# Attention behind a group norm: the first batch's keys as centred input, the scale folded into weights and z

## The reference

```python
xg = x.reshape(B, 4, C // 4, H, W)
y = ((xg - mean(xg)) * rsqrt(var(xg) + 1e-5)).reshape(B, C, N) * gamma + beta
q, k, v = split(w_qkv @ y + b_qkv, 3)
scores = q.T @ k * C ** -0.5
out = x + w_out @ (softmax(scores) @ v.T).T + b_out
```

## Time and profile before

| | us |
|---|---|
| median of 3 runs | 136.11 |
| lowest, highest | 136.02, 136.78 |
| the profiled execution | 135.91 |
| its span, first to last instruction | 134.1 |
| PE busy | 129.0 |
| DVE busy | 100.1 |
| ACT busy | 74.8 |
| POOL busy | 73.0 |

### The profile page before, as it was taken

One profiled execution on the slowest core, in us unless ns is written; L12 is line 12 of the kernel. 1 busy time (PEld: TensorE's weight loads), 2 busy tenths in 40 slices (PEclk: granted clock), 3 DMA queues, 4 the chain that ended last, 5 costly groups with the idle time before them and its releaser, 6 DMA issues.

```text
span 134.1 us, 1876 instructions
## 1 busy us (share of the span) xinstructions
PE 129.0 (96%) x579; PEld 91.1 (68%) x579; DVE 100.1 (75%) x191; ACT 74.8 (56%) x131; POOL 73.0 (54%) x78
## 2 busy tenths in 40 slices
PE   6999999999999999999999999999999999899991
PEld 6877687777777566666765656776665676558890
DVE  0598686999999999769788785698886826759121
ACT  3164768775588655656753284576732545868000
POOL 6133166589458877963386678933493355142600
PEclk9999999999999999999999999999999999999999
DMA  4950000000039808596799458963898299902111
GB/s 158 332 215 0 0 5 0 0 2 0 0 78 207 187 0 196 131 210 175 163 210 209 122 117 194 215 185 86 191 209 221 51 209 210 229 9 78 39 65 52
DMA packets 6874, 16.63 MB, mean 124 GB/s; under 512 B 1873, under 2 KB 2129, under 8 KB 6865
## 3 DMA queue, kind: packets, MB, share of 16 engines
q1 hardware_dynamic: 6576, 16.26, 49.4%
q10 hardware_dynamic: 288, 0.27, 0.6%
HBM read 2.36 MB, written 2.10 MB: 33 GB/s over the span
## 4 chain that ended last, share of the span: by engine, by line
PE 73%; DVE 9%; POOL 7%; issue 4%; DMA 2%; ACT 1%; POOLq 0%; DVEq 0%
PE mixed L847 22%; PE scores L793 8%; PE scores L794 8%; PE scores L796 8%; DVE scores L592 4%; PE turned L810 4%; POOL probs L334 4%; PE turned L740 3%; DVE crossed L619 3%; DMA xs<-in_x_dram 2%; PE mixed L849 2%; POOL y_lo L310 2%; PE mixed L740 1%; DVE stats L518 1%; PE mixed L844 1%
## 5 line engine op out<-in xcount | busy, mean ns | idle before, releaser
L334 POOL TENSOR_SCALAR probs<-probs,inv_sum 128x1024 f32<-128x1024 f32 x32 | 35.9, 1122 | 42.0 <-DVE inv_sum L597 41.9
L592 DVE TENSOR_SCALAR_CACHE_REDUCE scores<-scores,key_bias 128x1024 f32<-128x1024 f32 x31 | 40.0, 1289 | 11.5 <-PE scores L796 11.5
L421 ACT ACTIVATE probs<-scores,neg_max 128x1024 f32<-128x1024 f32 x32 | 35.7, 1116 | 20.0 <-DVE scores L592 19.2
L847 PE MATMUL mixed<-crossed,v 128*128 128x512 f32 x84 | 39.5, 592 | 0.0
L793 PE MATMUL scores<-y_hi,z_hi 128*128 128x512 f32 x62 | 34.5, 557 | 0.1
L619 DVE STREAM_TRANSPOSE crossed<-probs 128x1024 f32<-128x1024 f32 x24 | 29.8, 1242 | 1.4 <-POOL probs L334 1.2
L794 PE MATMUL scores<-y_lo,z_hi 128*128 128x512 f32 x62 | 24.4, 394 | 0.0
L847 PEld LDWEIGHTS mixed<-crossed,v 128*128 128x128 f32 x84 | 15.1, 190 | 11.0 <-issue 10.1
L796 PE MATMUL scores<-y_hi,z_lo 128*128 128x512 f32 x62 | 19.3, 392 | 0.0
L793 PEld LDWEIGHTS scores<-y_hi,z_hi 128*128 128x128 f32 x62 | 11.7, 189 | 8.5 <-issue 5.7
L794 PEld LDWEIGHTS scores<-y_lo,z_hi 128*128 128x128 f32 x62 | 11.7, 189 | 7.0 <-issue 5.5
(11 more groups left out here) (159 smaller groups left out, 179.5 us busy)
## 6 DMA issues: line engine op xcount, KB each, us to landing
crossed<-crossed SPq DMA_DIRECT2D x92, 128.0 KB, 2.3
out_dram<-result SPq DMA_DIRECT2D x7, 256.0 KB, 2.4
xs<-in_x_dram SPq DMA_DIRECT2D x2, 512.0 KB, 6.7
xs<-in_x_dram SPq DMA_DIRECT2D x3, 256.0 KB, 4.8
xs<-in_x_dram ACTq DMA_DIRECT2D x1, 256.0 KB, 3.3
ws<-in_weights_dram SPq DMA_DIRECT2D x1, 256.0 KB, 3.6
out_dram<-result SPq DMA_DIRECT2D x2, 128.0 KB, 1.9
vecs<-in_vectors_dram ACTq DMA_DIRECT2D x1, 3.0 KB, 3.8
```

What stands on the lines that cost most here:

```text
L334: pool.tensor_scalar(probs[:, i % RING, :], probs[:, i % RING, :], inv_sum[:, i:i + 1], 1.0, ALU.mult, ALU.mult).then_inc(s_probs, 1)
L421: act.activation(probs[:, i % RING, :], scores[:, i % 2, :], ACT.Exp, bias=neg_max[:, i:i + 1], scale=-1.0, accum_out=row_sum[:, i:i + 1]) ...
L592: dve.tensor_scalar(scores[:, i % 2, :], scores[:, i % 2, :], key_bias[:, b % 2, i:i + 1], None, ALU.subtract, ALU.min, accum_out=neg_max[ ...
L847: mm = pe.matmul(bank, v[:, b % 2, k, :], at, start=first, stop=final)
```

## The change

For batch 0 alone, z and the scores no longer use the normalised input but c = x less its channel mean. The normalised input is norm_a * c + shift, where shift = norm_a * (channel mean less group mean) + beta. Of z = G y + z_bias the scale on the input side goes into the fold (`first_fold_hi`, `first_fold_lo`: the fold times norm_a along its rows), the shift's product with the fold into the bias, and the scale on the key side into z, which is multiplied by norm_a as ACT copies it (`scale=norm_a`, `first_z_bias`). So the heads of the keys need only the channel means. The key bias of batch 0 gets a column of its own in `wv_out` (C + 1, from `first_key_vector`) and a scalar of its own (`first_bias_score`), since the queries' side changes with the shift; PE gets four one-column products for this (lines 978, 989, 999, 1007 of the new kernel), DVE and ACT some one-column instructions. The values are still made of the normalised input y: ACT makes 384 columns, POOL 640.

The z tail of the second half stands between the second normalisation and the input of batch 1. The core of the diff (lines unchanged in kind are left out):

```diff
@@ gpsimd @@
-            pool.tensor_scalar(minus_mean[:, :], group_mean[:, :], -1.0, None, ALU.mult).then_inc(s_const, 1)
...
+            pool.wait_ge(s_c1, 1)
+            pool.wait_ge(s_c_hi, 2)
+            pool.wait_ge(s_c_lo, 2)
+            pool.tensor_tensor(y_lo[:, 0, second], y[:, 0, second], y_hi[:, 0, second].bitcast(fp32),
+                               ALU.subtract).then_inc(s_c_lo_rest, 1)
...
+            first_z_tail(1, FIRST, HALF)
             pool.wait_ge(s_norm, 1)
+            pool.wait_ge(s_c_lo_rest, 1)
+            pool.tensor_scalar(y[:, 0, 3 * 128:N], xs[:, 0, 3 * 128:N], norm_a[:, 0:1], norm_b[:, 0:1],
                                ALU.mult, ALU.add).then_inc(s_y0_rest, 1)
...
+            pool.tensor_tensor(fold_lo[:, :], fold[:, :], fold_hi[:, :].bitcast(fp32), ALU.subtract).then_inc(s_fold_lo, 1)
             normalise(0, 0)
             rstd_of(1, 2, 2)
             normalise(0, 1)
+            first_z_tail(2, HALF, N)
@@ scalar @@
+            act.wait_ge(s_centre, 1)
+            for half in (slice(0, HALF), slice(HALF, N)):
+                act.activation(y_hi[:, 0, half], xs[:, 0, half], ACT.Identity, bias=centre[:, :]).then_inc(s_c_hi, 1)
             act.wait_ge(s_folded, 1)
+            act.activation(fold[:, :], setup[:, SET_G:SET_G + C], ACT.Copy, scale=-SCALE).then_inc(s_fold, 1)
...
+            act.wait_ge(s_folded, 3)
+            act.activation(wv_out[:, 0:C], setup[:, SET_V:SET_V + C], ACT.Copy).then_inc(s_setup, 1)
+            act.wait_ge(s_fold, 1)
+            act.wait_ge(s_scale, 1)
+            act.activation(first_fold_hi[:, :], fold[:, :], ACT.Identity, scale=norm_a[:, 0:1],
+                           bias=blank[:, 0:1]).then_inc(s_first_fold_hi, 1)
...
             def first_values(job, bank):
                 act.wait_ge(s_v0, V_NO[job] + 1)
+                act.wait_ge(s_key_bias, V_NO[job] + 1)
                 value_copy(0, job, bank)
@@ vector @@
+            dve.tensor_scalar(centre[:, :], mean_var[:, 0, 0:1], -1.0, None, ALU.mult).then_inc(s_centre, 1)
+            channel_spreads(0, 1, mixed[:, 1, :])
...
+            centred_tail(1, slice(0, FIRST))
             variances(0, 1, 1, mixed[:, 1, :])
...
             def first_key_biases(job, bank):
-                dve.wait_ge(s_v, V_NO[job] + 1)
+                dve.wait_ge(s_v0, V_NO[job] + 1)
@@ tensor @@
-                pe.matmul(minus_means[:, MINUS_MEAN + lo:MINUS_MEAN + hi], minus_mean[:, :],
-                          mean_var[:, lo:hi, 0], start=True, stop=True).then_inc(s_gmean, 1)
...
+            pe.wait_ge(s_fold, 1)
+            pe.matmul(setup[:, SET_Z:SET_Z + 1], wqk[:, 1, :], BQ, start=True, stop=True).then_inc(s_folded, 1)
...
-            keep_warm(3)
+            keep_warm(2)
...
+            pe.matmul(mixed[:, 1, first], first_fold_hi[:, :], c_hi[:, first], start=True, stop=False)
+            pe.matmul(mixed[:, 1, first], first_fold_hi[:, :], c_lo[:, first], start=False, stop=False)
+            pe.wait_ge(s_first_fold_lo, 1)
+            pe.matmul(mixed[:, 1, first], first_fold_lo[:, :], c_hi[:, first], start=False, stop=True).then_inc(s_z0, 1)
```

More of the change, by code:

```diff
@@ new lines, in _ @@
+            act.wait_ge(s_first_biases, 1)
+            act.activation(wv_out[:, C + 1:C + 2], mixed[:, 0, FIRST_U:FIRST_U + 1], ACT.Copy, scale=SCALE).then_inc(s_setup, 1)
+            act.activation(z_full[:, FIRST:HALF], turned[:, 0, FIRST:HALF], ACT.Identity, scale=norm_a[:, 0:1],
+                           bias=first_z_bias[:, :]).then_inc(s_z0_full, 1)
+            act.wait_ge(s_first_biases, 2)
+            act.activation(first_bias_score[:, :], mixed[:, 1, FIRST_S:FIRST_S + 1], ACT.Copy, scale=SCALE).then_inc(s_setup, 1)
@@ L479, in _ @@
             exponentials(0, 1)
+            act.wait_ge(s_z0_tail, 1)
+            act.activation(z_full[:, :], mixed[:, 1, :], ACT.Identity, scale=norm_a[:, 0:1],
+                           bias=first_z_bias[:, :]).then_inc(s_z0_full, 1)
             for b in range(BATCHES):
@@ L902, in _ @@
[L902 to L907 removed]
+            c_hi, c_lo = y_hi[:, 0, :], y_lo[:, 0, :]
@@ L916, in _ @@
[L916 to L921 removed]
+            pe.matmul(to[0], z_hi[:, 0, first], c_hi[:, halves[0]], start=True, stop=False)
@@ new lines, in _ @@
+            pe.wait_ge(s_c_hi, 2)
+            pe.matmul(to[1], z_hi[:, 0, first], c_hi[:, halves[1]], start=True, stop=False)
+            pe.wait_ge(s_c_lo, 2)
+            pe.matmul(turned[:, 0, left], first_fold_hi[:, :], c_lo[:, left], start=False, stop=True).then_inc(s_z0, 1)
+            pe.matmul(to[0], z_hi[:, 0, first], c_lo[:, halves[0]], start=False, stop=False)
+            pe.wait_ge(s_first_key, 1)
+            pe.matmul(mixed[:, 0, FIRST_U:FIRST_U + 1], wqk[:, 0, :], first_key_vector[:, :], start=True,
+                      stop=True).then_inc(s_first_biases, 1)
```

279 lines of the change are left out of this document (159 added, 120 removed).

## The result

| | before | after |
|---|---|---|
| median of 6 runs each, us | 136.50 | 139.48 |
| lowest, highest | 136.02, 136.78 | 139.19, 140.60 |
| ratio, after to before | | 1.0239 (1.0201 to 1.0277) |
| the profiled execution, us | 135.91 | 140.60 |
| its span | 134.1 | 138.8 |

The changed kernel is 2.4% slower: 3.3 us by the ratio, 3.0 by the medians. The forecast was 136.5 with 137.3 as its upper bound. With three more runs the kernel before has a median of 136.50, where the forecast was worked out from 136.11. All ratios here are the record's; they leave out runs more than 1.5% above the fastest of the same kernel: 139.53 of the first experiment, 138.02 of the last but one, and of the kernel before one at 166.5 with a mean clock of 0.755.

What follows compares the result with a forecast made beforehand. The prediction saw an opening of dependent steps, then full DVE and PE queues from DVE's maximum of block 5 at 25.98 us. +0.87 − 0.19 − 0.22 = +0.46 gave 136.5 us, range 135.3 to 137.3.

Steps and rivals of the forecast that it cites:

- the sum: Whole kernel: +0.87 at block 5's maximum, −0.19 and −0.22 given back later, +0.46 us in all.
- the hinge: DVE's maximum of block 5, at 25.98 us before; delay there passes almost whole to the end; forecast 26.85, +0.87.
- step 5: Behind block 5's maximum: DVE's wait at 40.88 goes, −0.19 us, and the mean product at 60.06 goes, −0.22.
- the rival on the clock: PE idles about 0.75 before the setup products; its clock falls, some 1.5 us more, 138; chance 0.05.
- Step 1: Setup to first z: PE waits for the fold copy; first z product at about 9.15 against 8.83, 0.3 late.
- Steps 2 and 3: First scores, values, first exponential: last score product and first values 0.5 late, block 1's maximum about 0.65; earlier exponential buys nothing.
- Step 4: Blocks 2 to 5: value copies wait for the key bias, exponentials behind them; block 5's maximum +0.87 us.
- The first rival: Opening: scaled fold not held by setup products, all up to first z 0.65 earlier; 135.4 to 135.7; chance 0.2.
- The second: Blocks 2 and 3: exponentials held twice by ACT's V1 and V2 copies behind the key bias; +0.95, 137.1; chance 0.25.

Runs made afterwards that it cites:

- the first experiment: Changed kernel with three warming products ahead of PE's wait for the fold copy, against the kernel before: median 137.17 us, ratio 1.0049.
- the last but one: Kernel before with the later means subtracted, plus the first exponential ahead of the first value copy: 135.93 us, ratio 0.9969 against the kernel before.
- the warm kernel: Changed kernel plus one warming product where the second mean product stood and three ahead of the fold wait: 137.01 us, ratio 1.0045 against the kernel before.
- both moves on ACT: Changed kernel, fold copied between key halves, scaled fold ahead of the value-weight copy, warming products filling pauses: 136.48 us, ratio 0.9994 against the kernel before.
- V1 and V2 freed: Kernel with both moves on ACT and PE kept warm, only its first value copy still behind the key bias: 136.17 us, ratio 0.9980 against the kernel before.
- one short pause: Kernel with both moves on ACT, without the two warming products ahead of the fold wait: 139.11, 139.19, 138.96 and 136.03 us.

## Why the prediction was wrong

**The verdict.** Wrong, by a step that it named and priced away. Kept warm throughout, the change costs 0.45% (0.25 to 0.65), 0.6 us (0.8 by the medians), where the sum said 0.46. The other 1.9%, 2.6 us, goes with the half clock. It isn't a property of this change: the kernel before loses 2.4 us by a pause, 1.8 of them beyond the delay. That the sum comes so near the warm kernel is partly luck: at the hinge that kernel is 1.34 late and not 0.87, and behind it more is given back than the 0.41 of step 5.

**The step that failed: the rival on the clock.** The text said that PE would idle for about 0.75 before the setup products, that a fall of the clock there would make products up to about 11 us take twice as long, 1.5 us, and that "nothing in the trace speaks for it", and gave it a chance of 0.05. The pause came as written, 0.79. The chance was wrong: all 6 runs of the changed kernel had the half clock, and pauses of 0.34 to 0.55 brought it too. The price was wrong as well, 1.5 us where 2.6 were lost: the half clock lasted to 17.9 us in the profiled run, over the scores, the values and the next block's first product, and for 6.9 us in the shorter runs, which is past 14 if it fell where it did here. The reasoning took "granted clock is 1.00 in all stretches" as a sign that the clock is safe. The stretches of the earlier trace rows begin at 26 us and say nothing of the opening; the page does show 9 in every slice, but only for a kernel in which PE hardly pauses there. What did speak for the danger stood in the same trace: ten warming products in front and three in the middle keep PE fed, and its longest pause there is 0.19.

**Step 1** had the right string and sized it short: the first z was to be 0.32 late, and kept warm it is 0.81 late. (A slip in its sum has no weight: with 0.70 each and an overlap of 0.1 the halves end at 6.93, not 6.96.) The key halves were no part of the error: 0.70 was expected of each, and the group of them in the changed kernel (count, busy us, mean ns) reads

```profile
L492 ACT ACTIVATE y_hi<-xs,first_negated_means 128x512 fp32r<-128x512 f32 x2 | 1.3, 712 | 0.0
```

By the rule of the Trainium skill, "ScalarE: Activation LUTs", section "What ACT_TABLE_LOAD costs", it would be 0.71; the trace agrees. The five products started at 7.41 (7.2 expected). The extra warming products stand in the 0.81, since they end behind the fold copy (8.27 against 7.91), and the runs don't part the two. With both moves on ACT the scaled fold starts at 8.65.

**Steps 2 and 3** hold as differences. From the first z to the last score product the warm kernel loses 0.10 more, the first values add nothing, block 1's maximum 0.2 more; the text had 0.2, 0.0 and 0.15. That the earlier exponential buys nothing is shown by the kernel that has it alone.

**Step 4.** From block 1's maximum to the hinge the warm kernel loses 0.23, the text had 0.22. The place is right too: block 3's exponential runs to 25.85 there and PE's scores of block 5 start at 25.99, 1.06 behind the turning ahead of them, where the old opening takes 0.85 (23.84 to 24.69). With V1 and V2 freed it is 0.85 again (23.75 to 24.60), and 0.26 comes back at the hinge of that profile.

**Step 5.** The removed mean products give 0.54 us (0.34 to 0.76) in the old kernel, for 0.41. Beside that kernel, which has them removed as well, the warm one is 1.34 late at the hinge and 1.2 at the end of the span (135.5 against 134.3). In the changed kernel the hinge is 5.1 late and the span 4.7 longer, and the reciprocal no longer waits.

**The first rival** (the opening flies) fell: the fold copy held PE, as the text said against it. **The second** (exponentials held twice, 137.1) has its time by chance near the warm kernel's 137.01, but not its mechanism: block 1's maximum was already 1.1 late, and block 2's exponential ends at 22.67, before PE is ready for block 4's scores at 23.23, so only one exponential holds PE.

**What is left.** The best of the kernels here is the old opening with the later means subtracted, 0.996 (0.9944 to 0.9975). With both moves, no pause and free value copies the new opening reaches 0.998 (0.9962 to 0.9998), so of the forms tried here none pays beyond the subtraction that it brings.

## What to carry to other kernels

Before adding a wait to TensorE near a kernel's start, look up its longest pause there so far, and treat any longer one as a danger to the clock, not as free idle time: here pauses of 0.34 to 0.79 us made kernels 2.4 to 3.3 us slower in most runs, the delay itself included. Fill the wait with products on a blank tile: the same delay with the pause filled cost 0.6 us in place of 2.4. A clock that reads 1.00 everywhere speaks for the present order, and says nothing about the next.

## What the hardware showed

**Short pauses, a long half clock.** After pauses of 0.34 to 0.79 us, the last of them ending between 6.6 and 7.4 us, the granted clock fell from 1.00 to 0.50 within 0.2 to 2.8 us, and stayed there for 6.8 us in five traces and 10.3 in one, though PE is busy for 0.99 or more of each whole stretch in it. The Trainium skill, "TensorE: Matmul & The Clock Gate", section "Why this matters for your kernels", warns of idle gaps between bursts of matmuls, but only of far longer ones. Here a single gap of 0.34 us was enough in three of four runs, and the measurement decides.

**The column of the clock at the start.** In the kernel before the granted clock reads 1.00 from the first stretch on, while its ten warming products (20 records) take 0.20 us a record:

```profile
1.04 4.06 PE L873 MATMUL scores<-blank 128*128 128x128 f32 x20 [1.04 <-DVE blank L642]
```

The three that follow at 7.73 take 0.15 a record (0.91 for six). From start to start the comparison is sharper. In the kernel with the pause filled, six records follow one another in 0.67 us at a granted 1.00 (9.10 to 9.77), 0.11 each; in the one with the pause open, six take 1.28 at 0.50 (8.94 to 10.22), 0.21 each. In the kernel with the subtraction alone the twenty at the start take 4.43 us (1.04 to 5.47), 0.22 each, and in the kernel before 3.89, 0.19 each. So the warming products run at the pace of the lower level, for longer in some executions than in others, and this moves the start of the opening by some half a microsecond between profiles. A column of 1.00 is no proof of full speed at a program's start.

**The same program, two outcomes.** The kernel with one short pause ran at 138.96 to 139.19 three times and once at 136.03; the one with warming in the pause had runs at 0.975, 0.987 and 1.00, from 139.53 down to 136.60. A pause of this kind can make a kernel's times scatter by 2%, and a median of few runs then tells little. On a smaller scale, the warm form of the changed kernel took 136.62 to 136.80 in its five runs with a mean clock of 0.997 to 0.999, and 136.88 to 137.50 in the seven at 1.00. Why the lower mean goes with the shorter time was not settled.
